# Two channel-attention stages of a twelve-stage decoder kernel: one product for values and sums, a turned division, row groups in pairs, and a root on GpSimd

## Chip, core and metric

The kernel runs on one core of one Trainium2 chip. The metric is the time of one execution on the device, in microseconds (us), as the median of the runs. TensorE multiplies matrices into PSUM (eight banks of 512 float columns on 128 partitions), VectorE and ScalarE work elementwise and read PSUM, GpSimd works on SBUF alone, SyncE issues the loads. The engines run side by side and wait for one another through semaphores.

## The reference, cut to the two stages

The whole is a decoder of twelve layers over x (16 batches of 128 rows and 256 columns) with layer norms between. The change touches layers 8 and 11 (stages 7 and 10, counted from 0), both attention over channels against the same context:

```python
def _L2_xattn_ref(q, k, v):                 # _L3_xattn_ref: the same, times gamma
    N_HEAD = 8
    qh = q.reshape(b * h, d // h, m)        # 128 rows into 8 heads of 16; m = 256
    kh = k.reshape(b * h, d // h, -1)
    vh = v.reshape(b * h, c // h, -1)
    qk = jnp.einsum('bdm,bdn->bmn', qh, kh) * scale      # 256 x 256 per head, scale 1/4
    sm = jax.nn.softmax(qk, axis=-1)
    ret = jnp.einsum('bmn,bcn->bcm', sm, vh)
    return ret.reshape(b, c, m)

x = _layernorm(x + _L2_xattn_ref(x, ctx_2048, ctx_2048), axis=-1)
x = _layernorm(x + _L3_xattn_ref(x, ctx_2048, ctx_2048, L3_xattn_gamma), axis=-1)
```

## The kernel before

Each layer is a class (`Stage`). A stage yields its steps from one generator, `order()`, and each of the four engines walks through the same list and emits its own part of each step. The order of the instructions on every engine is thus written by hand, and semaphore counts (`Signal`) join the engines. `STAGES` lists the layers; `Channels` is stage 7 and `ChannelsGamma` stage 10. Latent comes before stage 7 and Ternary after it; Scan before stage 10 and Quant after it.

**Layout.** A batch lies with its 128 rows on the partitions, so a head is 16 partitions and a *row group* of 32 partitions (r = 0 to 3) holds two heads, e = 0 and 1. GpSimd makes masked copies: XE (x, the partitions of the other head at zero) and KE (the context likewise, with ones at one partition of the other head). The free partitions carry the negative maximum later, so that one matmul gives score minus maximum.

**A batch goes through these steps.** "s": scores, XE as weights and KE as moving data, 32 partitions deep and 256 columns wide, four row groups at once into banks 0 to 3, in two halves k (128 of the queries each); VectorE takes the negative maxima of each bank (`hMX`, L2967). "sh": TensorE turns the maxima (L2887), VectorE adds them into XE (L2973). "t": the scores again, turned, with the maximum in them (L2899), two row groups at a time, k = 0 to 3, in banks 4 and 5; ScalarE takes the exponential into E (L2937). "vt": TensorE turns the context (L2867), ScalarE copies it (L2930), GpSimd masks it into VE (L3023). "o": E times VE (L2912, 32-wide weights, four column groups at once), then E times a masked matrix of ones (`hone`, L2912) in two parts, which gives each sum of a row on the 16 partitions where the result stands. ScalarE copies both (L2943). "mul": VectorE inverts the 256 sums on all partitions (L2979), multiplies (L2984, or L2982 with gamma) and adds x (L2987).

Every fp32 matmul leaves two records in the trace, so 16 matmuls are "x32" there; a transpose leaves one.

**The pipeline.** Iteration t of `order()` holds "s" and "sh" for batches t and t-1, "t" for t-1, "o" for t-2 and "mul" for t-3. The norm of four batches follows in three steps (statistics, root, scaling), each in an iteration of its own; the root is twelve dependent operations on 128x4 (`rsqrt`, `rsqrt_rest`, L196 to L214). `ASIDE` puts steps of the next stage into given iterations: the preparation of Ternary's first four batches in iterations 16 and 17, Quant's weight rounding and its first group in iterations 3 to 16.

## Time and profile before

| | us |
|---|---|
| median of 3 runs | 4110.23 (4107.7 to 4121.14) |
| span of the profiled execution | 4117.8 |
| TensorE busy | 3583.7 (87%) |
| VectorE busy | 3057.9 (74%) |
| ScalarE busy | 1939.7 (47%) |
| GpSimd busy | 1167.6 (28%) |
| stage 7, first key to last scaling | about 2455 to 2667 |
| stage 10, likewise | about 3757 to 4008 |

The profile's page gives the busy time of each engine, and the span in forty slices with the TensorE clock that was granted. Busy is not the same as needed: an engine can be busy while nobody waits for it, so the timeline of single iterations and the waits say more. The two stages touched are some 465 us of 4118.

### The profile page before, as it was taken

To read this page: it belongs to the slowest core of one execution; us is meant where nothing else is said; L and a number is where in the kernel's file an instruction comes from. 1 tells how busy PE (TensorE), PEld (TensorE's weight loads), DVE (VectorE), ACT (ScalarE), POOL (GpSimd) and SP (SyncE) were. 2 spreads that over 40 slices of the span, in tenths; PEclk is the share of its full clock that TensorE was granted. 3 is DMA by queue.
4 is the path that set the end of the run, shared out by engine and by line. 5 is a ranking of instruction groups with operands and counts; after the bars stand their busy time and mean duration, and the time that the engine had idled before them with its cause. 6 is when DMAs were issued, how large, how long until landed. Compare 5 with 4: busy or idle time off the path is not lost. (4 is left out here: it accounts for less than half of the span.)

```text
span 4117.8 us, 65960 instructions
## 1 busy us (share of the span) xinstructions
PE 3583.7 (87%) x23747; PEld 2223.2 (54%) x23762; DVE 3057.9 (74%) x6508; ACT 1939.7 (47%) x4746; POOL 1167.6 (28%) x1208
## 2 busy tenths in 40 slices
PE   7799999998981777879999979888999999997885
PEld 3466666665661345645455545465655656564543
DVE  7788988988658675543455657868988898885678
ACT  4466666665532333311333324435656656563445
POOL 2533213334302000000111122114656555553210
PEclk9899999999995888889899988999999999997877
DMA  2222222222200100020000000022212211221000
GB/s 70 65 66 67 60 62 65 66 56 56 61 14 31 34 1 24 2 76 1 22 1 1 1 31 2 27 92 83 77 68 77 72 72 72 67 79 63 2 1 21
DMA packets 240594, 185.94 MB, mean 45 GB/s; under 512 B 117648, under 2 KB 216592, under 8 KB 239184
## 3 DMA queue, kind: packets, MB, share of 16 engines
q1 hardware_dynamic: 240272, 181.73, 14.7%
q8 instruction: 192, 3.15, 0.3%
q14 instruction: 130, 1.06, 0.1%
HBM read 166.45 MB, written 15.20 MB: 44 GB/s over the span
## 5 line engine op out<-in xcount | busy, mean ns | idle before, releaser
L310 PE MATMUL ps<-xT,min 128*128 128x512 f32 (+1 forms) x1072 | 503.0, 614 | 30.7 <-DVE macc L3349 30.3
L3349 DVE SCALAR_TENSOR_TENSOR macc<-ps,mcw,macc 128x508 f32<-128x508 f32 (+2 forms) x408 | 302.1, 741 | 81.2 <-ACT macc L3276 71.3
L3431 POOL TENSOR_TENSOR mSQ<-mSQ,mtn 128x512 f32<-128x512 f32 x128 | 240.2, 1877 | 362.1 <-ACT mtn L3301 362.0
L310 PEld LDWEIGHTS ps<-xT,min 128*128 128x128 f32 (+1 forms) x1072 | 191.9, 191 | 250.6 <-issue 204.3
L3424 POOL TENSOR_TENSOR mE<-mE,mCB 128x1024 f32<-128x1024 f32 x128 | 302.3, 2362 | 44.5 <-DVE mE L3359 26.5
L3359 DVE TENSOR_TENSOR_SCAN mE<-mE,mid 128x1024 f32<-128x1024 f32 x128 | 296.9, 2319 | 0.0
L3209 PE MATMUL ps<-mwo,macc 128*128 128x256 f32 x1024 | 244.5, 382 | 5.4 <-DVE macc L3366 5.3
L2937 ACT ACTIVATE hE<-ps 128x512 f32<-128x512 f32 x256 | 139.0, 595 | 223.5 <-PE ps L2899 223.5
L2351 POOL TENSOR_TENSOR lP<-lP,lm 128x512 f32<-128x512 f32 x64 | 66.6, 1041 | 574.5 <-DVE lm L2324 574.5
L3297 ACT ACTIVATE mtn<-ps,mcol 128x64 f32<-128x64 f32 x1024 | 222.9, 334 | 2.9 <-PE ps L3188 2.8
L826 POOL TENSOR_TENSOR dTB<-did,dNB 128x1024 f32<-128x1024 f32 (+1 forms) x10 | 28.7, 2869 | 662.6 <-DMA dNB<-d_N 598.4
L2260 ACT ACTIVATE lP<-ps,lm 128x128 f32<-128x128 f32 x256 | 90.6, 366 | 266.1 <-DVE lm L2320 266.1
L2967 DVE TENSOR_REDUCE hMX<-ps 128x2 f32<-128x512 f32 x256 | 158.8, 683 | 58.8 <-PE ps L2878 58.7
L3209 PEld LDWEIGHTS ps<-mwo,macc 128*128 128x128 f32 x1024 | 186.1, 192 | 28.7 <-DVE macc L3366 8.2
L732 DVE SCALAR_TENSOR_TENSOR dav<-ps,dsmall,dav 128x508 f32<-128x508 f32 (+2 forms) x192 | 142.3, 741 | 46.7 <-ACT dav L603 42.1
L2899 PE MATMUL ps<-hXE,hKE 32*128 32x256 f32 x1024 | 165.3, 445 | 12.9 <-DVE hXE L2973 7.9
L831 POOL TENSOR_TENSOR dTB<-dTB,dtmp 128x30 f32<-128x30 f32 (+11 forms) x300 | 168.7, 562 | 23.5
L732 DVE SCALAR_TENSOR_TENSOR daq<-ps,dsmall,daq 128x508 f32<-128x508 f32 (+2 forms) x192 | 142.3, 741 | 42.5 <-ACT daq L603 37.0
L830 POOL TENSOR_TENSOR dtmp<-dNB,dTB 128x30 f32<-128x30 f32 (+11 forms) x300 | 155.9, 520 | 23.5
L732 DVE SCALAR_TENSOR_TENSOR dak<-ps,dsmall,dak 128x508 f32<-128x508 f32 (+2 forms) x192 | 142.1, 740 | 25.3 <-ACT dak L603 20.7
L502 PE MATMUL ps<-dKQ 128*128 128x256 f32 x512 | 138.3, 397 | 25.9 <-ACT dO L678 17.3
L2161 PE MATMUL ps<-lCQ,lq 128*128 128x512 f32 (+1 forms) x256 | 142.6, 656 | 17.8 <-DVE lQA L2315 17.8
(581 smaller groups left out, 8470.9 us busy)
## 6 DMA issues: line engine op xcount, KB each, us to landing
mE<-m_decay SPq DMA_DIRECT2D x128, 512.0 KB, 3.6
dwk<-in_L_attn_Wk SPq DMA_DIRECT2D x64, 128.0 KB, 2.3
dwq<-in_L_attn_Wq SPq DMA_DIRECT2D x64, 128.0 KB, 2.4
dwv<-in_L_attn_Wv SPq DMA_DIRECT2D x64, 128.0 KB, 2.4
dwg<-in_L_attn_Wg SPq DMA_DIRECT2D x64, 128.0 KB, 2.4
dwo<-in_L_attn_Wo SPq DMA_DIRECT2D x64, 128.0 KB, 2.6
min<-in_m_in SPq DMA_DIRECT2D x2, 4096.0 KB, 18.5
d_N<-dNT SPq DMA_DIRECT2D x256, 16.0 KB, 1.5
```

Of the source, the lines that this page charges most:

```text
L310: t = pe.matmul(out, w[:, j, :], self.c.xT[:, j, blk(g, 512)], start=j == 0, stop=j == 1)
L732: x = dve.scalar_tensor_tensor(out=acc[:, :, 3 - j:T], in0=p[:, :, 0:T - 3 + j], scalar=small[:, 4 * k + j:4 * k + j + 1], in1=acc[:, :, 3 ...
L830: then(pool.tensor_tensor(part, bc(NB[:, s, s + 1:32], s, True), bc(TB[:, s, 0:s], 31 - s), ALU.mult))
L831: then(pool.tensor_tensor(low, low, part, ALU.subtract))
L2899: t = pe.matmul(bank(4 + i)[:, blk(lt, 256)], self.KE[x][r, e, blk(lt)], self.XE[x][r, e, :], start=True, stop=True)
L2967: m = dve.tensor_reduce(self.MX[y][:, k, 32 * r:32 * r + 32:16], bank(r).rearrange("p (e n) -> p e n", e=2), AX.X, ALU.max, negate=True)
L3209: t = pe.matmul(bank(to + j // 2)[:, blk(j % 2, 256)], self.acc[s][:, blk(j)], self.wo[:, i, :], start=i == 0 and j % 2 == 0, stop=i == 31 ...
L3297: x = act.activation(self.tn[s][:, h], bank(6)[:, h], ACT.Copy, scale=self.col[:, 4 * g + j, 2 * i + e:2 * i + e + 1])
L3349: x = dve.scalar_tensor_tensor(out=acc[:, :, 3 - j:T], in0=p[:, :, 0:T - 3 + j], scalar=self.cw[:, i, j:j + 1], in1=acc[:, :, 3 - j:T], op ...
L3359: dve.tensor_tensor_scan(E, E, self.id8[:, :, :].rearrange("p b t -> p (b t)"), 0.0, ALU.mult, ALU.add).then_inc(*self.de.up)
L3424: pool.tensor_tensor(E, E, bc(self.CB[g % 2][:, :, :].rearrange("p b t -> p (b t)"), 2), ALU.mult).then_inc(*self.em.up)
L3431: pool.tensor_tensor(self.SQ[g % 2][:, :], self.SQ[g % 2][:, :], self.tn[s][:, :], ALU.add).then_inc(*self.sqa.up)
```

## The change

It rewrites the class `Channels` (and with it `ChannelsGamma`).

- **One product for both sums.** The weights of "o" are now 16 columns of values and 16 columns of ones for each head (VE, 32 wide). Each head has its own half of bank 6. The product with `hone` is gone, and with it the load of `c_rowpar` and the masked copies on GpSimd: ScalarE writes the turned context straight into the value columns; the ones are set once, on VectorE.
- **Turned result.** ScalarE copies bank 6, TensorE turns it in four transposes ("ot"), VectorE inverts 16 sums per partition and multiplies; TensorE turns the quotient back in two transposes ("back"), and VectorE adds x (times gamma where there is one).
- **Paired row groups.** "s" now has four parts of two row groups, each next to the part of "t" on the other two. "s" rotates through banks 0 to 2, "t" through 3 to 5; each bank is handed back by a count of its own.
- **Norm.** Statistics follow batch by batch ("stat"); aggregation and scaling stand at two places between the maxima of later batches (`norm_step`); the root is an addition and a power of -0.5 on GpSimd (`norm_pool`).
- **Pipeline.** "t" now belongs to batch t-2, "o" to t-3, "back" to t-4; XE and KE have four buffers. The aside steps stand at the end of an iteration.

```diff
     def buffers(self):
         c = self.c
-        self.KE, self.XE, self.VE, self.V, self.MX, self.E, self.O = (c.sets(n, "h" + m, *z) for n, m, *z in (
-            (3, "KE", 2, D), (3, "XE", 2, D), (3, "VE", 2, 2, 128), (2, "V", 2, 128), (2, "MX", 2, 128), (2, "E", 8, 2, D), (2, "O", 2, D)))
-        self.R, self.P1 = [c.R, c.f32("hR", 4, D)], c.f32("hone", 2, 128)
+        self.KE, self.XE, self.VE, self.MX, self.E, self.O, self.Y, self.rd = (c.sets(n, "h" + m, *z) for n, m, *z in (
+            (4, "KE", 2, D), (4, "XE", 2, D), (2, "VE", 2, 4, 2, 32), (2, "MX", 2, 128), (2, "E", 8, 2, D), (2, "O", 512), (2, "Y", D), (2, "rd", 16)))
...
     def order(self):
 
-        yield "vt", 0, 0
-        for t in range(NB + 3):
-            for step, b, k in (("sh", t - 1, 0), ("s", t, 0), ("mul", t - 3, 0), ("t", t - 1, 0), ("o", t - 2, 0), ("t", t - 1, 1), ("s", t, 1),
-                               ("o", t - 2, 1), ("t", t - 1, 2), ("vt", t + 1, 0), ("o", t - 2, 2), ("t", t - 1, 3)):
+        yield "keys", 0, 0
+        for t in range(NB + 4):
+            for step, b, k in (("keys", t + 1, 0), ("stat", t - 5, 0), ("t", t - 2, 0), ("s", t, 0), ("sh", t - 1, 0), ("vt", t - 2, 0),
+                               ("t", t - 2, 1), ("s", t, 1), ("o", t - 3, 0), ("t", t - 2, 2), ("s", t, 2), ("ot", t - 3, 0),
+                               ("t", t - 2, 3), ("s", t, 3), ("back", t - 4, 0)):
                 if 0 <= b < NB:
                     yield step, b, k
-                if step == "s" and k == 1:
-                    for n, first in (("stats", 6), ("rsqrt", 7), ("scale", 8)):
-                        if t >= first and (t - first) % 4 == 0:
-                            yield n, (t - first) // 4, 0
-                    if t in self.ASIDE:
-                        yield "aside", *self.ASIDE[t]
-        yield "rsqrt", 3, 0
-        yield "scale", 3, 0
+            if t in self.ASIDE:
+                yield "aside", *self.ASIDE[t]
+            if t == NB:
+                yield "norm", 2, 0
+        yield "stat", NB - 1, 0
+        yield "norm", 3, 0
...
+    def norm_step(self, dve, own, g, k):
+
+        c = self.c
+        if k == 0:
+            dve.wait_ge(own.sem, self.last)
+            if g:
+                dve.wait_ge(*self.rq.at(g))
+            for j in range(4):
+                x = dve.bn_aggr(c.st[:, j, 6:8], c.st[:, j, 0:6])
+            x.then_inc(*self.var.up)
+        else:
+            dve.wait_ge(*self.rq.at(g + 1))
+            c.scale_vector(dve, g, self.R[g % 2])
+
+    def norm_pool(self, pool, own, g):
+
+        c = self.c
+        pool.wait_ge(*self.var.at(g + 1))
+        o = own(pool.tensor_scalar(self.pw[:, 0:4], c.st[:, :, 7:8].rearrange("p a b -> p (a b)"), 1e-5, 1.0, ALU.add, ALU.mult))
+        pool.wait_ge(own.sem, o)
+        pool.tensor_tensor(c.rsq[:, 0:4], self.pw[:, 0:4], self.pw[:, 4:8], ALU.pow).then_inc(*self.rq.up)
...
-            x, y = b % 3, b % 2
+            x, y = b % 4, b % 2
+            banks = [(8 * b + 2 * k + i) % 3 + (3 if step == "t" else 0) for i in range(2)]
...
             elif step == "s":
                 if k == 0:
                     pe.wait_ge(*self.xe.at(b + 1))
                     pe.wait_ge(*self.ke.at(b + 1))
-                for r in range(4):
-                    pe.wait_ge(*room[r])
+                for n in banks:
+                    pe.wait_ge(*room[n])
                 for e in range(2):
-                    for r in range(4):
-                        t = pe.matmul(bank(r)[:, blk(1 - e, 256)], self.XE[x][blk(r, 32), e, blk(k)], self.KE[x][blk(r, 32), e, :],
-                                      start=True, stop=True)
+                    for i, n in enumerate(banks):
+                        r = blk(2 * (1 - k % 2) + i, 32)
+                        t = pe.matmul(bank(n)[:, blk(1 - e, 256)], self.XE[x][r, e, blk(k // 2)], self.KE[x][r, e, :], start=True, stop=True)
                 t.then_inc(*self.sc.up)
-                for r in range(4):
-                    room[r] = self.mx.at(2 * b + k + 1)
+                for i, n in enumerate(banks):
+                    room[n] = self.mx.at(8 * b + 2 * k + i + 1)
...
+                for n in banks:
+                    pe.wait_ge(*room[n])
                 for lt in range(2):
-                    for i in range(2):
+                    for i, n in enumerate(banks):
                         r = blk(2 * rr + i, 32)
-                        t = pe.matmul(bank(4 + i)[:, blk(lt, 256)], self.KE[x][r, e, blk(lt)], self.XE[x][r, e, :], start=True, stop=True)
+                        t = pe.matmul(bank(n)[:, blk(lt, 256)], self.KE[x][r, e, blk(lt)], self.XE[x][r, e, :], start=True, stop=True)
                 t.then_inc(*self.tr.up)
-                for i in range(2):
-                    room[4 + i] = self.ex.at(4 * b + k + 1)
+                for i, n in enumerate(banks):
+                    room[n] = self.ex.at(8 * b + 2 * k + i + 1)
             elif step == "o":
-                if k == 0:
-                    pe.wait_ge(*room[6])
-                    pe.wait_ge(*self.ve.at(b + 1))
-                    pe.wait_ge(*self.ex.at(4 * b + 4))
-                for e in ((0, 1), (0,), (1,))[k]:
+                pe.wait_ge(*room[6])
+                pe.wait_ge(*self.ve.at(b + 1))
+                pe.wait_ge(*self.ex.at(8 * b + 8))
+                for e in range(2):
                     for lt in range(2):
                         for r in range(4):
-                            w = self.P1[:, e, blk(r, 32)] if k else self.VE[x][:, lt, e, blk(r, 32)]
-                            t = pe.matmul(bank(6)[blk(r, 32), blk(min(k, 1), 256)], w, self.E[y][:, 2 * r + e, lt, :], start=e + lt == 0,
-                                          stop=e + lt == 2)
-                if k == 2:
-                    t.then_inc(*self.o.up)
-                    room[6] = self.oc.at(b + 1)
+                            t = pe.matmul(bank(6)[blk(r, 32), blk(e, 256)], self.VE[y][:, lt, r, e, :], self.E[y][:, 2 * r + e, lt, :],
+                                          start=lt == 0, stop=lt == 1)
+                t.then_inc(*self.o.up)
+                room[6] = self.oc.at(b + 1)
+            elif step == "ot":
+                pe.wait_ge(*room[6])
+                for n in range(4):
+                    t = pe.transpose(bank(6)[:, blk(n)], self.O[y][:, blk(n)], c.ident[:, :])
+                t.then_inc(*self.ot.up)
+                room[6] = self.mul.at(b + 1)
+            elif step == "back":
+                pe.wait_ge(*room[7])
+                pe.wait_ge(*self.mul.at(b + 1))
+                for qt in range(2):
+                    t = pe.transpose(bank(7)[:, blk(qt)], self.Y[y][:, blk(qt)], c.ident[:, :])
+                t.then_inc(*self.bk.up)
+                room[7] = self.sum.at(b + 1)
...
+                    act.wait_ge(*self.o.at(b - 1))
+                act.copy(self.VE[y][:, :, :, :, 0:16].rearrange("p l r e c -> p (l r) e c"),
+                         bank(6)[:, 0:256].rearrange("p (w e c) -> p w e c", e=2, c=16)).then_inc(*self.ve.up)
...
-            elif step == "o" and k == 2:
+                    n = (8 * b + 2 * k + i) % 3 + 3
+                    act.activation(self.E[y][:, 2 * (2 * rr + i) + e, :, :], bank(n).rearrange("p (n q) -> p n q", n=2), ACT.Exp,
+                                   scale=0.25).then_inc(*self.ex.up)
+            elif step == "o":
...
         dve.wait_ge(*self.c.xn.at(4 * self.n))
+        dve.wait_ge(*self.prev.ended())
         dve.wait_ge(self.dma[0], 32)
         for e in range(2):
             r = own(dve.tensor_reduce(self.row[:, e:e + 1], c.ident[:, 16 * (1 - e)::32], AX.X, ALU.add))
         for y in range(2):
             r = own(dve.memset(self.MX[y][:, :, :], 0.0))
+            o = dve.memset(self.VE[y][:, :, :, :, :].rearrange("p l r e c -> p (l r e c)"), 1.0)
+        o.then_inc(*self.row1.up)
         dve.wait_ge(own.sem, r)
-        dve.wait_ge(self.dma[4], 32)
-        dve.tensor_copy(self.P1[:, :, :], self.rp[:, :, :]).then_inc(*self.row1.up)
...
+                for i in range(2):
+                    n, r = (8 * b + 2 * k + i) % 3, 32 * (2 * (1 - k % 2) + i)
+                    dve.tensor_reduce(self.MX[y][:, k // 2, r:r + 32:16], bank(n).rearrange("p (e n) -> p e n", e=2), AX.X, ALU.max,
+                                      negate=True).then_inc(*self.mx.up)
+                    late, w = (b - 8) % 4, 2 * k + i - 1
+                    if b >= 8 and w >= 0 and 7 * late + w in (0, 12):
+                        self.norm_step(dve, own, (b - 8) // 4, 7 * late + w)
+            elif step == "stat":
+                dve.wait_ge(*self.sum.at(b + 1))
+                self.last = own(dve.bn_stats(c.st[:, j, 0:6], self.R[g % 2][:, j, :]))
...
+            elif step == "ot":
+                dve.wait_ge(*self.ot.at(b + 1))
+                p = bank(6).rearrange("p (e w h c) -> p e w h c", e=2, h=2, c=16)
+                rd = self.rd[y][:, :].rearrange("p (e w) -> p e w", e=2)
+                if b >= 2:
+                    dve.wait_ge(*self.bk.at(b - 1))
+                r = own(dve.reciprocal(rd, p[:, :, :, 1, 0]))
                 dve.wait_ge(own.sem, r)
+                dve.tensor_tensor(self.Y[y][:, :].rearrange("p (w e c) -> p e w c", e=2, c=16), p[:, :, :, 0, :],
+                                  rd.unsqueeze(3).broadcast_to([128, 2, 8, 16]), ALU.mult).then_inc(*self.mul.up)
+            elif step == "back":
+                R = self.R[g % 2][:, j, :]
...
+                    a = dve.tensor_tensor(R, bank(7)[:, 0:256], c.X[:, b, :], ALU.add)
+                a.then_inc(*self.sum.up)
...
+            if step == "norm":
+                self.norm_pool(pool, own, b)
+            elif step == "s" and k == 1 and b >= 8 and b % 4 == 0:
+                self.norm_pool(pool, own, b // 4 - 2)
+            elif step == "keys":
...
                 i.then_inc(*self.ke.up)
-                pool.wait_ge(*self.vk.at(b + 1))
-                if b >= 3:
-                    pool.wait_ge(*self.o.at(b - 2))
-                for e in range(2):
-                    i = pool.tensor_tensor(self.VE[x][:, :, e, :], self.V[b % 2][:, :, :], bc(self.rp[:, e, :], 2), ALU.mult)
-                i.then_inc(*self.ve.up)
```

TensorE, one iteration of the steady part of stage 7. ident turns; hMX are the maxima, hctx the context, hE the exponentials. Before:

```order
L2887 MATMUL ps<-ident_51,hMX_334_382 128x128 x2
L2878 MATMUL ps<-hKE_323_371,hXE_326_374 128x256 x8
L2899 MATMUL ps<-hXE_328_376,hKE_325_373 128x256 x4
L2912 MATMUL ps<-hE_337_385,hVE_330_378 32x256 x16
L2899 MATMUL ps<-hXE_328_376,hKE_325_373 128x256 x4
L2878 MATMUL ps<-hKE_323_371,hXE_326_374 128x256 x8
L2912 MATMUL ps<-hE_337_385,hone_389 32x256 x8
L2899 MATMUL ps<-hXE_328_376,hKE_325_373 128x256 x4
L2867 MATMUL ps<-ident_51,hctx_366 128x128 x2
L2912 MATMUL ps<-hE_337_385,hone_389 32x256 x8
L2899 MATMUL ps<-hXE_328_376,hKE_325_373 128x256 x4
```

The same place after the change (hO is the copied result, hY the quotient):

```order
L2908 MATMUL ps<-ident_51,hMX_332_380 128x128 x2
L2888 MATMUL ps<-ident_51,hctx_366 128x128 x2
L2920 MATMUL ps<-hXE_329_377,hKE_325_373 128x256 x4
L2900 MATMUL ps<-hKE_323_371,hXE_327_375 128x256 x4
L2931 MATMUL ps<-hE_334_382,hVE_330_378 32x256 x16
L2920 MATMUL ps<-hXE_329_377,hKE_325_373 128x256 x4
L2900 MATMUL ps<-hKE_323_371,hXE_327_375 128x256 x4
L2938 MATMUL ps<-ident_51,hO_336_384 128x128 x4
L2920 MATMUL ps<-hXE_329_377,hKE_325_373 128x256 x4
L2900 MATMUL ps<-hKE_323_371,hXE_327_375 128x256 x4
L2945 MATMUL ps<-ident_51,hY_339_387 128x128 x2
```

The two products with ones are gone, the eight-matmul score pieces are four of four, each behind a "t" piece, and six transposes are new.

VectorE, one iteration of stage 7 before (hXE takes the shift; L2979 is the reciprocal):

```order
L2967 TENSOR_REDUCE hMX_335_383<-ps 128x2 x4
L2979 RECIPROCAL hO_338_386<-hO_338_386 128x256
L2984 TENSOR_TENSOR R_57<-hO_338_386 128x256
L2987 TENSOR_TENSOR R_57<-R_57,X_49 128x256
L2967 TENSOR_REDUCE hMX_335_383<-ps 128x2 x4
L2973 SCALAR_TENSOR_TENSOR hXE_328_376<-ps,hpar_367,hXE_328_376 128x256 x2
```

And after, in the iteration in which a norm begins (L2862):

```order
L3004 TENSOR_REDUCE hMX_332_380<-ps 128x2 x2
L2862 BN_AGGR st_58<-st_58 128x2 x4
L3015 SCALAR_TENSOR_TENSOR hXE_329_377<-ps,hpar_367,hXE_329_377 128x256 x2
L3004 TENSOR_REDUCE hMX_332_380<-ps 128x2 x4
L3024 RECIPROCAL hrd_341_389<-ps 128x16
L3026 TENSOR_TENSOR hY_339_387<-ps,hrd_341_389 128x2x8x16
L3004 TENSOR_REDUCE hMX_332_380<-ps 128x2 x2
L3034 TENSOR_TENSOR hR_390<-ps,X_49 128x256
L3011 BN_STATS st_58<-hR_390 128x6
```

The division now stands between the third and the fourth part of the maxima, and the addition and the statistics between the last maxima of one batch and the first of the next.

## Rows read from the trace of the kernel before

**Rows 1.** The page: the span, and busy time of TensorE.

```profile
span 4117.8 us, 65960 instructions
PE 3583.7 (87%) x23747; PEld 2223.2 (54%) x23762; DVE 3057.9 (74%) x6508; ACT 1939.7 (47%) x4746; POOL 1167.6 (28%) x1208
```

**Rows 2.** Windows: stretch, length, busy per engine, clock, DMA share, GB/s.

```profile
2454.00:2489.00 35.00, 24.69 (x160) 15.67 (x160) 15.29 (x30) 6.06 (x12) 12.20 (x22) 0.50 0.26 91
2489.00:2643.00 154.00, 149.36 (x1804) 89.15 (x1798) 128.29 (x244) 71.29 (x137) 42.39 (x74) 0.99 0.01 2
3793.00:3974.00 181.00, 165.13 (x1794) 96.83 (x1790) 135.24 (x263) 80.98 (x145) 48.42 (x77) 0.89 0.01 1
```

**Rows 3.** Timeline, one warm iteration: start, length, engine, line, names, idle before.

```profile
2563.86 1.15 PE L2878 MATMUL ps<-hKE,hXE 32*128 32x256 f32 x16
2564.89 1.13 PE L2899 MATMUL ps<-hXE,hKE 32*128 32x256 f32 x8
...
2565.07 2.48 DVE L2967 TENSOR_REDUCE hMX<-ps 128x2 f32<-128x512 f32 x4 [0.23 <-PE ps L2878]
...
2565.96 1.93 PE L2912 MATMUL ps<-hE,hVE 128*32 128x256 f32 x32
...
2567.82 0.48 PE L2899 MATMUL ps<-hXE,hKE 32*128 32x256 f32 x2
...
2567.85 0.48 PE L2878 MATMUL ps<-hKE,hXE 32*128 32x256 f32 x2
...
2569.75 1.07 PE L2912 MATMUL ps<-hE,hone 128*32 128x256 f32 x16
...
2571.93 1.08 ACT L2937 ACTIVATE hE<-ps 128x512 f32<-128x512 f32 x2 [1.84 <-PE ps L2899]
...
2573.18 1.13 PE L2899 MATMUL ps<-hXE,hKE 32*128 32x256 f32 x8
...
2574.24 0.44 PE L2887 MATMUL ps<-ident,hMX 128*128 128x128 f32 x2
...
2574.61 1.15 PE L2878 MATMUL ps<-hKE,hXE 32*128 32x256 f32 x16
```

**Rows 4.** Timeline: first scores of batch 4, and last maxima turned, stage 7.

```profile
2506.89 1.15 PE L2878 MATMUL ps<-hKE,hXE 32*128 32x256 f32 x16
...
2640.80 0.44 PE L2887 MATMUL ps<-ident,hMX 128*128 128x128 f32 x2
```

**Rows 5.** Groups by line: shapes, count, busy us, mean ns, idle before.

```profile
L2967 DVE TENSOR_REDUCE hMX<-ps 128x2 f32<-128x512 f32 x108 | 67.0, 682 | 8.9 <-PE ps L2878 8.8
L2973 DVE SCALAR_TENSOR_TENSOR hXE<-ps,hpar,hXE 128x256 f32<-128x256 f32 x28 | 12.2, 477 | 16.9 <-PE ps L2887 16.9
...
L1869 DVE RECIPROCAL xrc<-ps 128x16 f32<-128x16 f32 x16 | 4.1, 256 | 15.9 <-PE ps L1738 15.9
...
L2333 DVE TENSOR_TENSOR R<-ps,X 128x256 f32<-128x256 f32 x16 | 5.7, 416 | 9.7 <-PE ps L2196 9.7
```

**Rows 6.** Timeline, end of stage 7: the root's first step, the last scaling.

```profile
2663.37 0.17 DVE L196 TENSOR_SCALAR rsq<-st 128x4 f32<-128x4 f32 x1
...
2665.75 1.38 DVE L246 TENSOR_SCALAR X<-hR,st,rsq 128x256 f32<-128x256 f32 x4
```

**Rows 7.** Groups of GpSimd by line and shape, whole span.

```profile
L3431 POOL TENSOR_TENSOR mSQ<-mSQ,mtn 128x512 f32<-128x512 f32 x128 | 240.2, 1877 | 362.1 <-ACT mtn L3301 362.0
...
L830 POOL TENSOR_TENSOR dtmp<-dNB,dTB 128x30 f32<-128x30 f32 x12 | 3.5, 294 | 0.9
```

**Rows 8.** Timeline, start of stage 10 at the lower clock.

```profile
3778.56 2.07 PE L2899 MATMUL ps<-hXE,hKE 32*128 32x256 f32 x8
...
3788.24 3.64 PE L2912 MATMUL ps<-hE,hVE 128*32 128x256 f32 x32
```

**Rows 9.** Timeline and windows, stage 7: an idle time of TensorE, and after.

```profile
2552.50 1.13 PE L2899 MATMUL ps<-hXE,hKE 32*128 32x256 f32 x8 [1.45 <-DVE hXE L2973]
...
2553.50:2557.50 4.00, 4.00 (x42) 2.06 (x42) 3.85 (x6) 1.08 (x2) 0.00 (x0) 0.57 0.00 0
```

78 lines of the change are left out of this document (29 added, 49 removed).

## The prediction, made before the changed kernel was run

> **What bounds the kernel now.** I read the page first: TensorE is busy for 87% of the span [rows 1], and the change touches two stretches of it, the two channel-attention stages. The view by windows then shows them [rows 2]: in the first, from 2489 to 2643 us, TensorE is busy for 149.4 of 154 us at a granted clock of 0.99, VectorE for 128.3; in the second, from 3793 to 3974 us, TensorE for 165.1 of 181 us at 0.89. Both begin with some 35 us at 0.50, the lower level (1.2 GHz). The timeline of one warm iteration (one batch in steady state) shows TensorE going from one group of matmuls to the next without an idle time over 0.41 us [rows 3]: from the first score product at 2563.86 to the same one of the next batch at 2574.61 is 10.75 us. With the norms the mean is larger: from 2506.89 to 2641.17 (the 2640.80 transposes plus 0.37) 12 iterations take 134.3 us, 11.19 each [rows 3, 4]. So TensorE is the bound, and VectorE, with 9.3 us of work in an iteration (128.3 over 13.8 of them), is close behind.
>
> **The pieces of the old iteration**, start to start [rows 3]: scores of half a batch (8 matmuls, 16 records, four row groups at once) 1.03; turned scores ("t", 4 matmuls, two row groups at once) 1.07, four times; value product 1.86; product with ones in two parts, 1.00 each; transposes of the maxima and of the context 0.37 each. The mixed piece at 2567.82 (a "t" and a half batch of scores) takes 1.93.
>
> **1. One product for both sums.** The value product keeps its 16 matmuls (1.86), the ones product goes: -2.0 us of TensorE per batch.
>
> **2. Paired row groups.** Scores now run on two row groups at a time, beside a "t" on the other two. Alone that would double them, from 4 x 0.26 to 8 x 0.26 us; paired they cost nothing beyond the "t". That both really run at once is in the trace: at 2567.82 and 2567.85 matmul records of both lines start within 0.03 us, though six more of the first line stand ahead of the second in the program [rows 3]. So a pair holds TensorE for 1.03 us and is complete 1.15 us after its start; four pairs are 4.1 us, where scores and "t" took 6.3. That is -2.2 us.
>
> The Trainium skill ("TensorE: Matmul & The Clock Gate", Part 3, what overlaps and what doesn't) says the opposite: matmuls start and end strictly in program order. By that rule the pair would take both lengths; it is rival B. The rows above speak against the rule.
>
> **3. Turned result.** Added on TensorE: four transposes of the result (0.74, as two pairs at 0.37) and two back (0.37). Sum of TensorE per batch: 4.12 + 1.86 + 0.74 + 0.37 + 0.37 + 0.37 = 7.8 us, against 10.75.
>
> **4. VectorE.** The 1.74 us reciprocal becomes one of 16 columns from PSUM; the nearest row is 0.26 [rows 5]. Multiply and add stay at 0.42 each, the maxima at 8 x 0.62, the shift at 2 x 0.44, statistics at 0.35 per batch [rows 3, 5]. Sum 7.3 us, plus what is left of the norm (0.38 + 1.37 per four batches) 0.4. The twelve small operations of the root went from 2663.37 to 2665.75, 2.4 us [rows 6]; they leave.
>
> **5. The hand-over is the new bound.** Scores rotate through three PSUM banks, "t" through three others. A pair needs two of each, so the next pair waits for the first evacuation of the last one. By the rows: complete at 1.15, VectorE starts 0.05 later, 0.68 for one maximum, 0.05 back, 1.93 us; by ScalarE 1.13 + 0.05 + 0.60 + 0.17 (the exp ends at 2573.01, the matmul starts at 2573.18) = 1.95 [rows 3, 5]. A pair thus starts at least 1.95 after the one before, though it holds TensorE for 1.03. What stands between the pairs fills this: two transposes (0.74) after the first, the product (1.86) after the second, which makes that step 2.9, the four transposes after the third, two after the fourth. Three steps of 1.95 and one of 2.9 are 8.75. VectorE is late for the first pair (it still has the last pair's second maximum, the add and the statistics), and the division between the third and fourth pair's maxima takes 0.7: step one becomes 2.1 and the last 2.05. I take **9.0 us**. The scaling of a group, 1.37, stands before the second maximum of the fourth pair, in iterations 9 and 13, and nothing hides it there: 2.8 us over 12 iterations. The aggregation (0.38) is hidden in VectorE's wait for the value product, some 1.4 us. Mean 9.2. Bounds: 7.8 (hand-over hidden) and 10.2 (each of the four steps 0.3 later).
>
> **6. GpSimd.** It loses the masked copies (0.73 each, x2) and gets an add and a power on 128x4. No row shows a power. The nearest rows are 0.29 for a 128x30 product and, at the far end, 1.88 for a 128x512 one [rows 7]; I take 0.3, nearest in size, with 0.2 for each hand-over. Before iterations 9 and 13 some 12 us of other work hide it. In the last two norms of a stage VectorE waits: under 1 us against 2.4 for the old chain. At 1.9 it would be 2 x 2 x 1.6 = 6 us more in all.
>
> **7. Start and filling.** VectorE now also sets the value buffers to one (two of 512 columns, about 0.54 each by the 0.27 for 256) ahead of GpSimd's first keys: +0.85 us. At the lower clock a lone step of scores takes 2.1 to completion as a "t" does [rows 8], and with 0.8 of hand-over an iteration is 4 x 2.9 = 11.6 us. The first begins at 2458.3. Three (the third 12.2, with its transposes) end at 2493.7. The fourth is longer for the value product (3.64 at this clock [rows 8]): 13 us, with the clock rising in it. Then iteration 4 begins at 2506.7; before, at 2506.89 [rows 4]. Zero. This assumes that the clock rises after the value product starts, as it did before.
>
> **8. Draining.** One stage deeper. From iteration 16 on: 8.8 + 8.8 for two iterations without scores, then product 1.9, copy 0.8, transposes 0.8, division 0.7, back 0.5, add 0.4, statistics and aggregation 0.8, root 0.9, scaling 1.4, together 25.8. In the first stage the next layer's first norm (5.6) and rounding (4.3) stand on VectorE between these and delay the last division by about 2.2. Sum 28.0 against 25.9 before (2641.2 to the end of the last scaling at 2667.1 [rows 4, 6]): +2.1.
>
> **Sum.** First stage: 0 - 12 x (11.19 - 9.2) + 2 = -22 us. Second stage the same -22 (its old draining ran partly at the lower clock; I count no gain there), plus about -4: some 40 us of its middle (181 x (1 - 0.89) x 2) run at the lower clock; a new iteration there takes 15.2: a pair holds TensorE for 2.0, and with 0.8 of hand-over, or the transposes (1.5), the product (3.4), the four transposes (1.4) in its place, the steps are 3.5, 5.4, 3.4 and 2.9. An old one, its pieces at this clock added up, takes about 19 [rows 8]. Together **-48 us**. The profiled span, 4117.8, becomes 4070; it is 7.6 above the median of the runs, so the median becomes 4110.2 - 48 = **4062 us**.
>
> **Rivals.**
>
> A, the other side: the clock. TensorE was busy without a break; now it idles about 0.8 us in every iteration and 1.5 to 2 us at each scaling. Before, an idle time of 1.45 us was followed by a fall to the lower level: 0.57 in the window from 2553.5 to 2557.5 [rows 9]. An iteration at the lower clock costs 15.2 instead of 9.2, 6.0 us. Ten more of the 24 such iterations give 4062 + 60 = 4122, from where the change is slower; if half of them are lost, 4134. Against it: the second stage's middle idled for 16 of 181 us and still was granted 0.89 [rows 2]. 0.07 for that much, 0.10 for two to six iterations lost (4074 to 4098 us), of it 0.03 within 0.3%.
>
> The Trainium skill describes this on the same page (the second failure mode, psum-queue depth-cycling): short idle times between groups that cycle through PSUM banks make the clock oscillate. By that rule the time would be A's. No row here shows it at gaps as small as 0.4 us.
>
> B: no overlap of the pair. A pair then holds TensorE for 2.1, an iteration is 4 x 2.1 + 1.86 + 1.85 = 12.1: 24 x 2.9 = 70 us more, 4132. The rows at 2567.8 speak against it. 0.03.
>
> C: the hand-over is hidden and the sum of TensorE decides, 7.8 to 8.2: 24 x 1.1 = 26 us less, 4036. The banks speak against it. 0.08.
>
> D: steps come later than I count or the power is slow (10.2 us per iteration, or 5 us per power): 4062 + 24 to 36, so 4086 to 4098. 0.10, of it half within 0.3%.
>
> **How the numbers follow.** Forecast 0.62 (4045 to 4080), A 0.17, B 0.03, C 0.08, D 0.10. A measurement of this kernel tells 0.3%, 12 us, from no change: faster is below 4098, slower above 4122. Faster: 0.62 + 0.08 + 0.07 of A + 0.05 of D = 0.82; same 0.03 of A and 0.05 of D = 0.08; slower 0.07 of A and B = 0.10. The range 4036 to 4098 leaves out the slower cases and parts of A, C and D, under 0.2.
>
> **What would show it.** The time between the transposes of the maxima in the warm part: 9.0 to 9.3 (C: 8.0; B: 12). Before each pair an idle time of TensorE of 0.1 to 0.5 us ended by the maxima or the exp. Matmuls of both lines starting together all through. Granted clock over 0.9 from iteration 4 on; if it is 0.75 or less, A. The power's duration on GpSimd, and VectorE's wait for it at the stage's end. If the stages shrink by 22 and 26 us and the time does not, something behind them gave it back. I am wrong first where the clock rises later than in iteration 3 or falls at each scaling.

## The result and the profile after

| | before | after |
|---|---|---|
| median | 4108.97 us (4 runs, 4097.44 to 4121.14) | 4056.61 us (4 runs, 4051.94 to 4061.73) |
| span of the profiled execution | 4117.8 us | 4054.3 us |
| stage 7, last scaling ahead of it to its own last | 213.1 us | 194.7 us |
| stage 10, likewise | 251.9 us | 215.6 us |

The ratio of the times is 0.9865, with a 95% interval from 0.9841 to 0.9889: faster, by 52 us, where 48 were forecast (median 4062, measured 4057). Of the 63.5 us between the two spans 18.3 lie in stage 7 and 36.3 in stage 10; 5.8 lie between the two stages and 3.1 outside, where the program is the same. A second profile of the changed kernel (below) has 5.6 us more between the stages than the first, so these are the spread of executions. The profiled execution before was also its slowest of the four (4121 us, 12 above the median), so the parts by stage add up to somewhat more than the 52 us of the medians.

The page, beside [rows 1]: TensorE lost 70 us of work and keeps its share, 87%. Its share of the span doesn't tell whether it is the bound.

```profile
PE 3513.2 (87%) x22915; PEld 2200.7 (54%) x22930; DVE 2995.6 (74%) x6414; ACT 1939.4 (48%) x4746; POOL 1137.0 (28%) x1162
```

The windows tell it, beside [rows 2] (stretch, length, busy time per engine with its count of instructions, granted clock, DMA share, GB/s): the start of stage 7, its warm part, the middle of stage 10.

```profile
2452.00:2497.00 45.00, 33.17 (x170) 21.95 (x170) 20.86 (x38) 6.17 (x12) 10.08 (x21) 0.50 0.20 70
2497.00:2640.00 143.00, 131.12 (x1528) 85.49 (x1524) 107.53 (x243) 78.70 (x149) 26.31 (x50) 0.97 0.01 2
3764.00:3917.00 153.00, 131.12 (x1496) 85.75 (x1496) 110.22 (x231) 85.60 (x155) 31.81 (x56) 0.97 0.01 1
```

In the warm part of stage 7 TensorE went from 149.4 busy of 154 us to 131.1 of 143: it now waits for 12 us there. The timeline of one warm iteration, beside [rows 3] (start, length, engine, line, names, idle time before it and what ended it; L2908 turns the maxima, once per batch):

```profile
2513.39 0.44 PE L2908 MATMUL ps<-ident,hMX 128*128 128x128 f32 x2
...
2513.98 0.70 PE L2920 MATMUL ps<-hXE,hKE 32*128 32x256 f32 x4
...
2515.40 1.93 PE L2931 MATMUL ps<-hE,hVE 128*32 128x256 f32 x32
...
2517.26 0.48 PE L2920 MATMUL ps<-hXE,hKE 32*128 32x256 f32 x2
...
2517.29 0.48 PE L2900 MATMUL ps<-hKE,hXE 32*128 32x256 f32 x2
...
2518.36 0.66 PE L2938 MATMUL ps<-ident,hO 128*128 128x128 f32 x4
...
2518.54 1.29 DVE L3004 TENSOR_REDUCE hMX<-ps 128x2 f32<-128x512 f32 x2 [1.74 <-PE ps L2900]
2519.19 0.48 PE L2920 MATMUL ps<-hXE,hKE 32*128 32x256 f32 x2 [0.17 <-ACT hE L2971]
...
2521.10 0.48 PE L2920 MATMUL ps<-hXE,hKE 32*128 32x256 f32 x2 [0.22 <-ACT hE L2971]
...
2522.45 0.44 PE L2908 MATMUL ps<-ident,hMX 128*128 128x128 f32 x2
```

From 2513.39 to 2522.45 is 9.06 us (10.75 before, 9.0 forecast). The scores (L2900) and the turned scores (L2920) start 0.03 us apart at 2517.26, and two pairs follow each other at 1.91 (2519.19, 2521.10), the hand-over of 1.95. By hand-over I mean the way from a bank that TensorE fills, through the engine that empties it, to the next matmul that may write there. Both of these pairs begin when ScalarE has emptied a bank ("<-ACT hE"). VectorE waits for 1.74 us before the third pair's maxima, which comes into use below.

An iteration with a scaling shows what the forecast had short. The scaling (L246) stands before the last maximum of the fourth pair; TensorE's next work waits for 1.32 us behind it, and the value product after it takes 3.54 us in place of 1.93, at a granted clock of 0.53:

```profile
2557.41 1.71 DVE L246 TENSOR_SCALAR X<-R,st,rsq 128x256 f32<-128x256 f32 x4
...
2560.10 0.44 PE L2908 MATMUL ps<-ident,hMX 128*128 128x128 f32 x2 [1.32 <-DVE hR L3034]
...
2562.33 3.54 PE L2931 MATMUL ps<-hE,hVE 128*32 128x256 f32 x32
...
2562.00:2565.60 3.60, 3.60 (x36) 1.38 (x32) 1.73 (x4) 0.95 (x2) 0.00 (x0) 0.53 0.02 5
```

The iteration with the scaling takes 10.44 us, and the one after it 10.89. At the second scaling of the stage the same happens (10.44, 10.38). The two ends of the twelve iterations, beside [rows 4]:

```profile
2504.34 0.44 PE L2908 MATMUL ps<-ident,hMX 128*128 128x128 f32 x2
...
2618.83 0.44 PE L2908 MATMUL ps<-ident,hMX 128*128 128x128 f32 x2
```

That is 114.5 us, 9.54 for each (11.19 before, 9.2 forecast). GpSimd's power is in the groups by line, and the end of the stage in the timeline, beside [rows 6, 7]: 1.02 us where 0.3 was taken, so that VectorE waits for 1.42 us between the aggregation and the scaling, where its own chain had taken 2.4.

```profile
L2874 POOL TENSOR_TENSOR rsq<-hpw 128x4 f32<-128x4 f32 x8 | 8.2, 1021 | 0.7
...
2644.30 1.01 POOL L2874 TENSOR_TENSOR rsq<-hpw 128x4 f32<-128x4 f32 x1
2645.35 1.38 DVE L246 TENSOR_SCALAR X<-hR,st,rsq 128x256 f32<-128x256 f32 x4 [1.42 <-POOL rsq L2874]
```

In stage 10 four iterations of 10.3 to 10.5 us at the full clock stand where stage 7 has 9.05. There four operations of 0.15 us from the weight preparation that runs beside this stage (line 2519 and on) stand behind the fourth pair's maxima, with a wait for a TensorE product ahead of them and the turning of the maxima behind:

```profile
3823.50 0.44 PE L2908 MATMUL ps<-ident,hMX 128*128 128x128 f32 x2
...
3832.80 0.16 DVE L2519 COPY qg<-ps 128x1 f32<-128x1 f32 x1 [0.47 <-PE ps L2415]
...
3833.80 0.44 PE L2908 MATMUL ps<-ident,hMX 128*128 128x128 f32 x2
```

Before, iterations of 10.75 us stood in stage 10 as in stage 7, so this work on VectorE was mostly free (the waits of the kernel before, 3809.6 to 3971.7, show TensorE waiting for it in four places, 8.9 us in all). Now it costs 1.2 us in an iteration like this one.

### The profile page after: what moved, and what is told of

Its sections match the earlier page's. It is cut to its first block and busy times, and to the rows that moved or that the text cites. A ratio compares the mean times of both kernels' runs of the same rounds, so it can differ in the third digit from the quotient of the medians.

```text
span 4054.3 us, 64218 instructions
## 1 busy us (share of the span) xinstructions
PE 3513.2 (87%) x22915; PEld 2200.7 (54%) x22930; DVE 2995.6 (74%) x6414; ACT 1939.4 (48%) x4746; POOL 1137.0 (28%) x1162
## 5 line engine op out<-in xcount | busy, mean ns | idle before, releaser
L2900 PE MATMUL ps<-hKE,hXE 32*128 32x256 f32 x1024 | 171.2, 456 | 40.6 <-issue 15.1
L2920 PE MATMUL ps<-hXE,hKE 32*128 32x256 f32 x1024 | 158.5, 428 | 20.2 <-ACT hE L2971 18.3
```

The costliest lines, as they stand in the source:

```text
L2900: t = pe.matmul(bank(n)[:, blk(1 - e, 256)], self.XE[x][r, e, blk(k // 2)], self.KE[x][r, e, :], start=True, stop=True)
L2920: t = pe.matmul(bank(n)[:, blk(lt, 256)], self.KE[x][r, e, blk(lt)], self.XE[x][r, e, :], start=True, stop=True)
```

## Experiments

Theory: the pair's two products run beside each other; the iteration is then set by the hand-over from pair to pair through VectorE and ScalarE; and TensorE's new idle times cost clock (bring it to the lower level) where they are long. Rivals stand with each run. "Iteration" is the time from one turning of the maxima to the next in stage 7's warm part, without a scaling.

| run | median us | ratio to before (95%) | iteration | stage 7 | stage 10 |
|---|---|---|---|---|---|
| changed kernel | 4056.6 | 0.9865 (0.9841 to 0.9889) | 9.05 | 194.7 | 215.6 |
| a0_after, the same | 4058.5 | 0.9876 (0.9853 to 0.9899) | 9.05 | 196.1 | 209.1 |
| e1_unpaired | 4172.3 | 1.0108 (1.0072 to 1.0145) | 11.11 | 228.0 | 287.9 |
| e2_back_twice | 4051.8 | 0.9859 (0.9844 to 0.9874) | 9.05 | 194.1 | 210.8 |
| e3_half_max | 4046.8 | 0.9845 (0.9818 to 0.9873) | 8.79 | 186.0 | 208.5 |
| e4_half_both | 4027.6 | 0.9803 (0.9773 to 0.9833) | 8.32 | 180.6 | 197.6 |
| b1_no_ones | 4127.4 | 1.0045 (1.0027 to 1.0063) | 10.20 | 223.1 | 250.8 |
| e6_root_vector | 4062.9 | 0.9880 (0.9864 to 0.9897) | 9.05 | 199.8 | 215.4 |
| e5_scale_early | 4054.8 | 0.9861 (0.9845 to 0.9876) | 9.05 | 188.9 | 209.5 |
| e7_both | 4054.9 | 0.9855 (0.9827 to 0.9883) | 9.05 | 188.9 | 209.9 |
| e8_warm | 4068.2 | 0.9888 (0.9867 to 0.9908) | 9.05 | 194.5 | 229.2 |
| e10_fill_early | 4035.9 | 0.9809 (0.9783 to 0.9836) | 9.05 | 175.0 | 209.6 |
| e11_fill_six | 4028.1 | 0.9789 (0.9767 to 0.9811) | 9.05 | 175.0 | 202.4 |

The stages are read from the profiled execution of each, while the median is that of all. Two executions of the changed kernel differ by 1.4 and 6.5 us in them, so a difference of stage 10 under some 7 us says nothing alone. b1_no_ones is an edit of the kernel before, all others of the changed kernel; e3, e4 and b1 leave out part of the softmax. The ten timed executions of the two together have their median at 4057.6.

### Do the pair's products run beside each other? (e1_unpaired)

```diff
-    r = blk(2 * (1 - k % 2) + i, 32)
+    r = blk(2 * (k % 2) + i, 32)
```

> One part of the change undone: a pair's first score tile and the transposes before it use the same row groups of the array, as in the kernel before, and nothing else is altered. If products on disjoint row groups really run beside each other (my theory), each of the two pairs of a batch's steps holds TensorE for about 1.0 us longer or hands over so much later, the steady iteration of 9.05 us becomes about 12, and 24 iterations give +65 to +75 us: 4120 to 4130 us. If the starts that the trace shows together are only how it records them (rival), TensorE runs in order either way and the time stays within 3 us of the changed kernel, about 4057 us.

(VectorE's maxima go to the place that belongs to the same row group by the same edit there, which is not shown.)

```profile
2527.11 0.44 PE L2908 MATMUL ps<-ident,hMX 128*128 128x128 f32 x2
...
2538.22 0.44 PE L2908 MATMUL ps<-ident,hMX 128*128 128x128 f32 x2
...
2538.81 1.13 PE L2920 MATMUL ps<-hXE,hKE 32*128 32x256 f32 x8
...
2539.77 1.03 PE L2900 MATMUL ps<-hKE,hXE 32*128 32x256 f32 x8
...
2540.73 1.93 PE L2931 MATMUL ps<-hE,hVE 128*32 128x256 f32 x32
```

(Timeline, one warm iteration. Line numbers are those of the kernel that is shown, here and below.) On the same row groups the second product starts when the first one's last matmul has (0.96 us later), and the pair holds TensorE for 1.92 us, where the changed kernel has both start 0.03 us apart. The overlap is real, and it is decided by the row groups. The iteration is 11.11 us, not the 12.1 that I had added up: the pair takes 1.92 and not 2.1, and all transposes together some 1.5 and not 1.85. Over 24 iterations 2.06 us are 49 us; measured are 115 by the medians (the profiled execution is 104 longer, 33 in stage 7 and 72 in stage 10), and the median lies outside the 4120 to 4130 that I had expected. The rest goes with the clock. Each scaling is followed by an iteration of 14.4 us, and stage 10 was granted 0.58 from 3840 to 3955:

```profile
3840.00:3955.00 115.00, 108.49 (x614) 68.95 (x612) 47.30 (x98) 32.52 (x59) 13.18 (x23) 0.58 0.00 1
```

Three of its nine executions took 4127.0 to 4130.7 us and six 4160.2 to 4177.5, the profiled one among the latter; the mean granted clock was 0.926 to 0.927 in the three and 0.915 to 0.919 in the six. So the same program can lose 40 us of clock or keep it; the 70 us that the three cost are the overlap's price with the scalings' part. This is the rival B of the prediction, and it was 4127 to 4177 instead of 4132.

The Trainium skill ("TensorE: Matmul & The Clock Gate", Part 3) says of matmuls on different row groups that they start and end strictly in program order. The changed kernel's trace differs: while six more records of L2920 (three matmuls) are to come, those of L2900, behind them in the program, already run.

### Hand-over or TensorE's work? (e2, e3, e4)

```diff
-    for qt in range(2):            # step "back"
+    for qt in (0, 1, 0, 1):
```

> The two transposes that turn the result back are issued twice in each batch, 0.37 us more of TensorE's work in each iteration, with the same output. If the iteration of 9.05 us is set by the chain of hand-overs between the maxima, the exponentials and the pairs (my theory), TensorE has that much time free and the kernel gains at most 3 us: 4057 to 4060 us. If TensorE's own work sets it (rival), every one of some 30 iterations grows by 0.37 us: +11 us, 4068 us.

```profile
2511.59 0.44 PE L2908 MATMUL ps<-ident,hMX 128*128 128x128 f32 x2
...
2518.63 0.66 PE L2945 MATMUL ps<-ident,hY 128*128 128x128 f32 x4
...
2520.64 0.44 PE L2908 MATMUL ps<-ident,hMX 128*128 128x128 f32 x2
```

Four transposes at 2518.63 for two, and 9.05 us from turning to turning: TensorE's added work is free, as the hand-over theory has it. It was smaller than I had expected, 0.22 us (0.66 for 0.44) and not 0.37, so that the rival's forecast would be some +7 us, 4064, and not 4068; measured are 4051.8.

```diff
-    dve.tensor_reduce(..., bank(n).rearrange("p (e n) -> p e n", e=2), ...)
+    dve.tensor_reduce(..., bank(n).rearrange("p (e n) -> p e n", e=2)[:, :, 0:128], ...)
```

> The channels' maxima are taken over half of the columns of each score tile, so part of the maximum's work is left out: each of the eight maxima of a batch takes 0.41 us in place of 0.68, 2.1 us less of VectorE's work in an iteration. If the iteration of 9.05 us is VectorE's throughput (rival), it falls towards 7.8 us, TensorE's sum: up to -1.2 us in 24 iterations, about -28 us. If it is the hand-over between pair, exponentials and the next pair (my theory), in which ScalarE's two exponentials of 0.6 us stay, the maxima of a pair are done before the exponentials and the iteration falls only by what the last of them was late, 0.2 to 0.4 us: -5 to -10 us.

```profile
L3004 DVE TENSOR_REDUCE hMX<-ps 128x2 f32<-128x256 f32 x90 | 34.2, 421 | 38.5 <-PE ps L2900 38.4
...
2504.62 0.44 PE L2908 MATMUL ps<-ident,hMX 128*128 128x128 f32 x2
...
2513.42 0.44 PE L2908 MATMUL ps<-ident,hMX 128*128 128x128 f32 x2
```

(Groups by line from 2497 to 2600, and timeline.) The maximum falls from 0.69 to 0.42 us, eight of them 2.1 us, and the iteration by 0.26: VectorE's throughput isn't the bound, it was only late by that much. Stage 7 is 8.7 us shorter: 3 from the twelve iterations, 3 from the start, where each step waits for a maximum, and 3 from the falls of the clock behind both scalings, which didn't come (the next iterations take 8.93 and 8.95, not 10.89 and 10.38), though TensorE still waited for 1.2 us at each scaling.

```diff
-    act.activation(self.E[y][:, 2 * (2 * rr + i) + e, :, :], bank(n)..., ACT.Exp, ...)
+    act.activation(self.E[y][:, 2 * (2 * rr + i) + e, 0, :], bank(n)[:, 0:256], ACT.Exp, ...)
```

> Maxima and exponentials both over half of the columns of each score tile (part of the softmax's work is left out; the product reads the half that is written, so that TensorE's work is the same). ScalarE's exponential falls from 0.59 to about 0.43 us and VectorE's maximum from 0.68 to 0.41. If the hand-over sets the iteration (my theory), its three steps of 1.95 us each lose two exponentials' 0.16 us and the lateness goes: 8.0 to 8.2 us, near TensorE's sum of 7.8: -20 to -26 us against the changed kernel. If something else sets it that neither engine's size touches (rival), the same as with the maxima alone.

```profile
L2971 ACT ACTIVATE hE<-ps 128x256 f32<-128x256 f32 x95 | 31.3, 381 | 39.8 <-PE ps L2920 39.8
...
2502.17 0.44 PE L2908 MATMUL ps<-ident,hMX 128*128 128x128 f32 x2
...
2510.50 0.44 PE L2908 MATMUL ps<-ident,hMX 128*128 128x128 f32 x2
```

The exponential falls from 0.59 to 0.38 us, and the iteration goes to 8.32: another 0.47. The whole is 4028, 30 us less, a little more than expected. Neither engine is busy all the time (ScalarE with 5.2 us of the 9.05), yet a shorter operation in the hand-over shortens the iteration. That leaves TensorE's sum (7.8 forecast) 0.5 below. The theory holds; for the iteration of 9.05 us TensorE's work alone and VectorE's work alone are both out as the bound.

### The first part alone, on the kernel before (b1_no_ones)

```diff
-    for e in ((0, 1), (0,), (1,))[k]:
+    for e in ((0, 1), (), ())[k]:
```

> The kernel before without the products with the matrix of ones (the row sums of the softmax are left out), and nothing else. TensorE's work falls by 2.0 us per batch from 10.2 to 8.2. If TensorE alone had set the iteration of 10.75 us (rival), it becomes 8.8 us in some 26 iterations: -50 us against the kernel before, 4059 us. If, as I worked out for the changed kernel, hand-overs and the other engines stand at about 9, a part of it is lost: 9.0 to 9.8 us, -25 to -45 us, 4065 to 4085 us.

```profile
2510.00:2550.00 40.00, 34.76 (x396) 22.73 (x398) 35.39 (x63) 20.05 (x40) 12.75 (x24) 1.00 0.01 2
...
3850.00:3960.00 110.00, 88.94 (x692) 53.05 (x688) 70.27 (x146) 42.19 (x72) 25.95 (x42) 0.71 0.01 1
```

The same window of the kernel before:

```profile
3850.00:3960.00 110.00, 99.23 (x1034) 57.20 (x1030) 78.90 (x157) 49.31 (x85) 27.65 (x44) 0.84 0.01 2
```

Both expectations were wrong, mine too: 2.0 us less work in each of 32 batches made the kernel slower by 17 us. The iteration fell by 0.55 only, to 10.2. In that window TensorE waits for 5.2 us in eight waits, 0.41 and 0.90 in each iteration, and all of them end when ScalarE has emptied a bank: the hand-over through the two banks of "t" sets the iteration here, not VectorE's work (35.4 of 40 us, with the 1.74 us reciprocal still in it). And the clock fell: 0.71 where it was 0.84, and in stage 7 six stretches at the lower level (34 us between 2493 and 2653) where before there were two (7 us). The first of them follows a wait of 2.5 us at a scaling; two more came behind it with no wait over 0.90. By the profiled executions stage 7 is 10 us longer and stage 10 1 us shorter, so in stage 10 the lost clock ate the gain. So the gain of this change doesn't come from leaving out the ones product by itself. That it needs the pairs is shown by e1_unpaired; that it needs the turned result, which takes the reciprocal off VectorE, is an argument: no run has it alone.

### The root on GpSimd (e6_root_vector)

```diff
-    x.then_inc(*self.var.up)
+    dve.wait_ge(own.sem, own(x))
+    self.root = c.rsqrt_of(dve, own, c.st, c.rsq, 1e-5)
```

> The second part of the change undone: VectorE works out the norm's reciprocal root by its own chain as in the kernel before, and GpSimd does nothing for it; the attention stays as changed. The power on GpSimd took 1.02 us, the sum before it 0.20, with a hand-over either way; VectorE's chain took 8 to 10 small operations. My theory: eight norms' roots, of which those inside the iterations add VectorE's time to the hand-overs and two stand at the stages' ends: +3 to +6 us against the changed kernel, 4060 to 4063 us. Rival: the two hand-overs and the slow power cost as much as VectorE's chain, no difference (within 2 us).

```profile
2538.35 0.44 PE L2903 MATMUL ps<-ident,hMX 128*128 128x128 f32 x2
...
2540.07 0.17 DVE L196 TENSOR_SCALAR rsq<-st 128x4 f32<-128x4 f32 x1
...
2549.02 0.44 PE L2903 MATMUL ps<-ident,hMX 128*128 128x128 f32 x2
```

4062.9 against 4057.6, as expected. The iteration with VectorE's chain takes 10.67 us, 1.6 more, in two places in stage 7 (its stage is 5.1 us longer). Though the power takes three times what I gave it, it is worth having where it is hidden, and worth 1 us at the end of stage 7.

At the end of stage 10 it costs 1 us. The last scaling of the changed kernel takes 3.39 us there and not 1.38, one of its four operations 2.42:

```profile
3942.42 2.34 POOL L2584 TENSOR_TENSOR X<-X,qb 128x1024 f32<-128x1024 f32 x1
3942.49 3.39 DVE L246 TENSOR_SCALAR X<-hR,st,rsq 128x256 f32<-128x256 f32 x4 [1.41 <-POOL rsq L2874]
```

GpSimd has an addition for the next layer (L2584) behind the power in its program; it has to wait with the power and then runs for 2.34 us beside the scaling. In e6_root_vector, where GpSimd doesn't wait for the root, it ran 38 us before the scaling (3918.04), and the scaling took 1.38. From the end of the aggregation to the end of the scaling that is 4.8 us with the power and 3.8 with VectorE's chain.

### The scaling where VectorE waits (e5_scale_early, e7_both, a0_after)

```diff
-    if b >= 8 and w >= 0 and 7 * late + w in (0, 12):
+    if b >= 8 and w >= 0 and 7 * late + w in (0, 9):
```

> VectorE's scaling by the channel norm stands three waits earlier in the iterations that have one, ahead of the third part's maxima, where the steady iteration shows VectorE idle for 1.74 us; the work is the same. If the 1.4 us by which those iterations are longer are the scaling on the path of the hand-overs, and if the stretches at the lower clock that follow both scalings of stage 7 come from TensorE's idle time there (my theory), 1.4 us go in each of four places and another 1.3 to 1.8 us behind two of them: -6 to -11 us against the changed kernel, 4046 to 4051 us. If VectorE has no free time there after all, or the root comes later than that place (rival), the delay only moves: within 3 us of it, or up to 4 us slower.

```profile
2551.73 0.44 PE L2908 MATMUL ps<-ident,hMX 128*128 128x128 f32 x2
...
2555.05 1.37 DVE L246 TENSOR_SCALAR X<-R,st,rsq 128x256 f32<-128x256 f32 x4
...
2560.79 0.44 PE L2908 MATMUL ps<-ident,hMX 128*128 128x128 f32 x2
```

The iteration with the scaling now takes 9.06 us for 10.44, the one after it 9.05 for 10.89, and stage 7 ends 5.8 us sooner (7.2 by a0_after). The scaling itself is shorter too, 1.37 us for 1.71: before, it ran beside GpSimd's masked copies, which took 1.38 us there and take 1.08 now. The two stretches at the lower clock behind the scalings are gone with TensorE's waits. The mechanism is as expected, though e3_half_max had the waits and not the falls. The total shows 3 us of it, 4054.8 against 4057.6, and the intervals overlap: measured is the stage, not the kernel.

> The changed kernel once more, so that the two versions beside it are compared with more executions of it and on the same chip: 4057 us, within 4 us. Its profile tells how far the stretches at the lower clock in stage 10 differ from one execution to the next: if they are set by the program alone (rival), the same iterations are long as before, 215.6 us for the stage; if chance has a part in them (my theory), stages 7 and 10 differ by some us.

4058.5 us. Stage 7 has the same iterations but for the two that follow a scaling (9.26 and 10.89 for 10.89 and 10.38): behind the same wait of 1.32 us the clock fell once and once not. Stage 10 has the same 129.0 us for its twelve iterations; all of its 6.5 us lie in the draining, 31.4 us for 37.9, where the first execution was granted 0.63 and this one 0.92. Chance has a part in the stretches at the lower clock.

> The scaling three waits earlier and the transposes back issued twice, together. The first alone left the steady iteration of 9.05 us also where the scaling stands and shortened stage 7 by 5.8 us in its trace, but fell behind in stage 10 in the iterations after the two short stretches at the lower clock; the second alone cost nothing in the iterations and had no such stretch in the first 150 us of stage 10. If TensorE's idle time is what lets the clock fall there (my theory), the two add up: 4046 to 4051 us. If the stretches come by chance (rival), it is the first edit's gain alone, 4052 to 4055 us.

4054.9 us; five of six executions lie from 4052 to 4056, one at 4026.3. Stage 7 is again 188.9, stage 10 has three stretches at the lower clock. The two edits don't add up; what e2_back_twice seemed to gain in stage 10 was within the spread.

### The start of a stage (e8_warm, e10_fill_early, e11_fill_six)

The largest stretch at the lower clock was left: the start, 45 us in stage 7 and 33 in stage 10 (35 and 37 before the change). TensorE has nothing to do from the last stage's end to the first scores.

```diff
+                if b == 0 and k == 0:
+                    pe.wait_ge(*room[6])
+                    for w in range(80):
+                        pe.transpose(bank(6)[:, blk(w % 4)], c.ident[:, :], c.ident[:, :])
...
+                if b < 2:
+                    for w in range(6):
+                        pe.transpose(bank(6)[:, blk(w % 4)], c.ident[:, :], c.ident[:, :])
```

> The changed kernel with work that computes nothing added on TensorE while both attention stages start: 80 transposes of the unit matrix into an idle bank before the first scores (some 9 us by the 0.109 us from one transpose to the next in the trace), and 6 after each score tile of the first two batches. In the changed kernel the clock stands at its lower level from 2449.6 to 2497.4 us, TensorE having done nothing from 2445 to 2456. If that is what the first two iterations of 11.81 and 12.01 us are (my theory), the clock stays up or rises at once, the first batch takes 8 in place of 12 us and the two iterations 8 to 9: -8 to -12 us in stage 7, somewhat less in stage 10, where the wait is 15 us and the added work doesn't fill it: -12 to -22 us in all, 4035 to 4045 us. Rival: the start is limited by GpSimd's preparation and by the hand-over of the maxima, and the clock falls in it anyway: no gain, or up to 5 us lost to the added transposes.

```profile
2446.24 8.90 PE L2895 MATMUL ps<-ident 128*128 128x128 f32 x80
2457.88 2.07 PE L2904 MATMUL ps<-hKE,hXE 32*128 32x256 f32 x8 [2.74 <-issue]
```

By the medians it lost 11 us, though the intervals overlap. In stage 7 the 80 transposes ran at the full clock (0.11 us each), ended 2.74 us before the first scores, and these took 2.07 us, the lower clock. From there on the added work cost time: from the stage's start to the fourth turning 54.9 us for 52.3. In stage 10, where the gap was 5.84 us, it was 57.8 for 48.4, the greater part of the loss. The next run closes the gaps: 104 transposes in stage 7 and 134 in stage 10, and 4 behind a score tile.

```diff
-                    for w in range(80):
+                    for w in range(104 if self.n < 9 else 134):
```

> Two edits on the changed kernel. The scaling stands three waits earlier, as measured before, and TensorE is kept at work through the start of both attention stages: 104 transposes of the unit matrix before the first scores of stage 7 and 134 in stage 10, and 4 behind each score tile of the first two batches. With 80 and 6 of them the transposes ran at the upper clock and ended 2.74 and 5.84 us before the first scores; in that idle time the clock fell, and the fill ran at the lower level as before, with the added work on top (+8 us against the changed kernel). By 0.109 us for each, 104 and 134 reach the first scores. If idle time of TensorE there is what lowers the clock (my theory), the first batch takes 8 in place of 12 us and the next two iterations 8 to 10: -10 to -20 us against the changed kernel, 4037 to 4047 us. If the clock falls whatever stands before the scores (rival), +5 us and the early scaling's gain: 4057 to 4062 us.

```profile
2440.88 11.52 PE L2895 MATMUL ps<-ident 128*128 128x128 f32 x104
2452.52 1.13 PE L2904 MATMUL ps<-hKE,hXE 32*128 32x256 f32 x8
...
3726.00:3746.50 20.50, 20.32 (x90) 12.61 (x86) 9.72 (x16) 1.14 (x1) 0.93 (x2) 0.50 0.03 12
```

4035.9 us, 22 less than the changed kernel and 19 less than with the early scaling alone. Now the first scores follow at once and take 1.13. The first two iterations of stage 7 are 7.5 and 8.0 us instead of 11.8 and 12.0, and the stage 175.0. In stage 10 the clock held for 5 us and fell at 3726.

> As the kernel with 104 and 134 transposes before the first scores, but 6 instead of 4 behind each score tile of the first two batches. In that kernel the clock stayed up through the whole start of stage 7 and fell in stage 10 at 3726.0 us, 5 us behind the first scores, with idle times of 0.29 to 0.39 us behind each tile. Two more transposes take 0.22 us of these. If the idle time that is left there is what lets the clock fall in stage 10 (my theory), it stays up there too: another -8 to -12 us, 4024 to 4028 us. If the fall comes by chance or from other work (rival), within 5 us of 4036 us, and the added transposes cost up to 1 us in each stage.

```profile
2447.00:2492.00 45.00, 41.83 (x419) 30.66 (x419) 29.58 (x55) 13.91 (x27) 12.04 (x25) 1.00 0.20 71
3716.00:3761.00 45.00, 41.13 (x352) 29.65 (x350) 27.41 (x49) 12.54 (x23) 12.03 (x25) 0.89 0.23 82
```

4028.1 us (ratio 0.9789, its interval below the changed kernel's): 2.1% faster than the kernel before, where the change alone gives 1.35%. The clock is at 1.00 over stage 7's start and at 0.89 over stage 10's, where the changed kernel had the lower level; it falls there at 3742, 6 us after the last of the added transposes. The gain over e10_fill_early is 8 us, 7.2 of them in stage 10; their intervals overlap (0.9783 to 0.9836 and 0.9767 to 0.9811). Of these two kernels the early scaling is a part; the filling without it was not run in this form, nor the filling on the kernel before.

## Why the prediction was right, step by step

- **The sum** was right: -48 forecast, -52.4 by the medians. By stages it was -22 and -26, measured -18.3 and -36.3. The mechanism held in both, but that the sum came so near is in part luck: in stage 10 a cost that was left out and a gain in clock that was priced too low stand against each other (below).
- **Steps 1 and 2** (one product, pairs) held: value product 1.93 us, both products starting together. By itself step 1 would have lost time (b1_no_ones), which the working, with its separate terms, could not show.
- **Step 3**, TensorE's sum: 7.8 us forecast. By the rows of e1_unpaired the transposes take 1.54 in all and not 1.85, which makes it some 7.5. It isn't the bound, so nothing hung on this.
- **Step 4**: VectorE's 7.3 us per iteration came out as 7.3 (32.4 us in 4.42 iterations, from 2510 to 2550).
- **Step 5**, the iteration: 9.0 forecast, 9.05 measured, and its cause shown from both sides (e2, e3, e4). Of its parts, three steps are a little shorter than forecast (1.9 us each for 2.1, 1.95 and 2.05) and the one with the product is longer, 3.3 for 2.9 (2513.98 to 2517.26), since the scores of the pair ahead of it start 0.36 us late; these errors cancel. The mean was mis-sized: 9.54 in stage 7 for 9.2. The scaling lengthened its iteration by 1.4, as priced (it took 1.71 beside GpSimd, for 1.37), but a fall of the clock followed it twice (10.89 and 10.38 in the next iteration), a mild form of rival A. +4 us.
- **Step 5 in stage 10** failed by an omission. The sum gave it stage 7's iteration, and its mean is 10.75 (129.0 us over 12): VectorE's operations for the weights beside it had mostly been hidden behind TensorE and now lie on the path, up to 1.2 us in an iteration. Against 9.2 that is 19 us too little. That the stage gained more than forecast all the same comes from the old iterations: their mean was not 11.2 but 13.5 (162.1 us), 28 us more, with single ones of up to 19.8. 41 us of the old middle ran at the lower clock, as I had read, and I let the new one have as much; it has 10. By an estimate from these two numbers, at half the clock, that is up to 15 of the 33 us that the twelve iterations gained. Why the new kernel kept its clock there is not shown, and only one execution of the kernel before was profiled.
- **Step 6**: the power takes 1.02 us, not 0.3, inside the bounds. The wait at the end is 1.42, not under 1. In an iteration it is hidden. What the working didn't see is the addition that waits on GpSimd behind the power: 2 us at the end of stage 10 (e6_root_vector).
- **Step 7**: zero in stage 7, as forecast (52.3 us for 52.4 from the stage's start to the turning at 2504.34). In stage 10 -4.8, since the clock rose 33 us after the start and not 37.
- **Step 8**: 27.5 us from the end of the last turning to the last scaling's end in stage 7, 28.0 forecast; +1.6 against before, +2.1 forecast. In stage 10 it was 37.9, again +1.6, but at the lower clock for most of it, before and after; the second execution took 31.4 there and 30.2 in stage 7. So this term has a spread of several us.
- **The rivals**: B and C are refuted, B with a price of 70 to 115 us and not 70. D's iteration of 10.2 us stands in stage 10 only, and by VectorE's other work and not by late steps. A came in its mildest form. Its large form exists: e1_unpaired and b1_no_ones are what it looks like. Of the psum-queue depth-cycling that the Trainium skill describes ("TensorE: Matmul & The Clock Gate", second failure mode) nothing was seen at idle times of 0.2 to 0.4 us (1.00 granted from 2510 to 2550); the two falls in stage 7's warm part came right behind the waits of 1.3 us. Such a wait is not enough by itself: it had no fall behind it once in a0_after, nor had one of 1.94 us in the kernel before (ended at 2599.21).

## What to carry to other kernels

When one engine is full and its work is cut, price the next bound as a chain, operation by operation from one hand-over to the next; then look for what the full engine had been hiding (a scaling, small operations for the next stage) and put it where the new timeline shows an engine waiting. Look also at what stands behind a wait in an engine's program: it is delayed with it. Cutting one engine's work alone can lose time, as b1_no_ones did by 17 us with less clock granted: change the balance as a whole. And look at the start of a stage: 104 and 134 transposes without use, reaching right up to the first real product, gave some 20 us here, and 80 of them with gaps of 2.7 and 5.8 us lost 11.

## What the runs showed of the hardware

- Matmuls on disjoint row groups of 32 rows overlap: two sets of 4 (8 records each) hold TensorE for 1.10 us together (2517.26 to 2518.36), and for 1.92 on the same row groups.
- GpSimd's power on 128x4 takes 1.02 us, and an addition on the same tile 0.20.
- VectorE and GpSimd can slow each other: the scaling of a group (four operations) takes 1.37 us alone and 1.71 beside two masked copies, which take 1.38 for 1.08; beside an addition of 128x1024 on GpSimd it takes 3.39.
- With 104 transposes in a row TensorE kept the granted clock at 1.00; an idle time of 2.74 us behind 80 of them was followed by the lower level, which then stayed from 2457.9 to 2488.6 us though TensorE was at work almost without a break.
- The same program can take two courses in its clock: e1_unpaired's executions lie in two groups 40 us apart.
